# A graph network's last layer: a place of its own on chip for each tile's result, and all 25 stores behind the last gather

## The reference

```python
for l in range(3):
    ht = einsum('nd,rdo->nro', h, W_rel[l])              # 16 relations
    h_rel = segment_sum(ht[src, etype], dst) + h @ W_loop[l] + b_rel[l]
    z = (h @ W_gat[l]).reshape(n, 4, 32)                 # 4 heads
    e = leaky_relu(sum(z * attn_l[l], -1)[src] + sum(z * attn_r[l], -1)[dst], 0.2)
    alpha = softmax of e over the edges of each dst
    h_gat = segment_sum(alpha * z[src], dst).reshape(n, D) + b_gat[l]
    hc = concatenate([h_rel, h_gat], 1) @ W_fuse + b_fuse
    if l == 0: hc = hc * sigmoid(concatenate([hc, mean(edge_weight)], 1) @ W_gate + b_gate)
    h = relu(hc)
return layernorm(x + h)                                  # rows of 128, eps 1e-5
```

## Time and profile before

| | |
|---|---|
| median of 3 runs | 3509.68 us (3509.45 to 3509.83) |
| the profiled execution | 3503.46 us |
| its span, first to last instruction | 3501.9 us |
| last layer's first gather | 2402.68 us |
| last layer's last gather starts | 3467.19 us |
| in-loop stores of the last layer, first and last start | 2515.19 us, 3457.57 us |
| last store starts | 3494.12 us |

### The profile page before, as it was taken

One profiled execution on the slowest core, in us unless ns is written; L12 is line 12 of the kernel. 1 busy time (PEld: TensorE's weight loads), 2 busy tenths in 40 slices (PEclk: granted clock), 3 DMA queues, 4 the chain that ended last, 5 costly groups with the idle time before them and its releaser, 6 DMA issues.

```text
span 3501.9 us, 18300 instructions
## 1 busy us (share of the span) xinstructions
PE 679.2 (19%) x1897; PEld 366.6 (10%) x1897; DVE 2383.4 (68%) x3251; ACT 424.3 (12%) x769; POOL 2488.3 (71%) x2642
## 2 busy tenths in 40 slices
PE   8832111222222220101121112211000000000000
PEld 5421000111111110000000001100000000000000
DVE  8536666677667755666667766674777777877787
ACT  4530111011111110111011111111000000000000
POOL 1557777777777747777777777775777777777774
PEclk9965555555555665555555555555555555555555
DMA  7874545455555544545455555554333333333332
GB/s 280 335 227 129 152 129 152 152 152 152 152 161 166 151 158 106 153 129 152 152 152 152 152 152 163 163 157 133 105 104 106 104 105 105 104 105 105 104 105 65
DMA packets 143244, 505.96 MB, mean 144 GB/s; under 512 B 44277, under 2 KB 51002, under 8 KB 133618
## 3 DMA queue, kind: packets, MB, share of 16 engines
q0 software_dynamic: 130032, 444.45, 43.6%
q1 hardware_dynamic: 13186, 61.24, 4.5%
HBM read 341.05 MB, written 164.51 MB: 144 GB/s over the span
## 4 chain that ended last, share of the span: by engine, by line
POOL 44%; issue 29%; DVE 12%; DMA 6%; PE 3%; POOLq 3%; DVEq 1%; SPq 1%; ACT 1%; ACTq 0%
POOL meta_nat L596 20%; POOL late L596 13%; POOL scratch L596 11%; DVE acc L1381 4%; DMA table<-rows 2%; DVE scratch L1377 1%; DMA scratch<-table,stage_tail 1%; DVE meta_nat L1377 1%; DMA late<-table,stage_mid 1%; PE ps_table L885 1%; DVE late L1377 1%; DMA meta_nat<-table,stage_head 1%; POOLq L369 1%; POOL table L675 1%; PE ps_cnt L918 1%
## 5 line engine op out<-in xcount | busy, mean ns | idle before, releaser
L596 POOL DMA_INDIRECT meta_nat<-table,stage_head x1200 | 1137.7, 948 | 394.5 <-issue 385.6
L596 POOL DMA_INDIRECT late<-table,stage_mid x720 | 681.5, 947 | 219.3 <-issue 216.5
L596 POOL DMA_INDIRECT scratch<-table,stage_tail x555 | 525.6, 947 | 171.1 <-issue 171.1
L1024 PE MATMUL ps_mix<-ident,hr 128*128 128x128 f32 x75 | 35.5, 473 | 2017.4 <-DVE hg L1401 2017.4
L787 ACT ACTIVATE ps_cnt<-logit 128x68 f32<-128x68 f32 x189 | 43.7, 231 | 2792.8 <-DVE logit L1363 2791.7
L1381 DVE TENSOR_REDUCE acc<-meta_nat 128x132 f32<-128x2112 f32 x75 | 290.6, 3875 | 7.7
L1371 DVE TENSOR_REDUCE acc<-meta_nat 128x128 f32<-128x2048 f32 x75 | 282.8, 3770 | 0.0
L1048 PE MATMUL ps_table<-wrel,hT 128*128 128x512 f32 x400 | 265.2, 824 | 0.0
L1353 DVE TENSOR_TENSOR raw<-late,er_cur 128x64 f32<-128x64 f32 x45 | 12.0, 267 | 337.4 <-DMA late<-table,stage_mid 337.4
L1024 PEld LDWEIGHTS ps_mix<-ident,hr 128*128 128x128 f32 x75 | 13.6, 181 | 2066.0 <-DVE hg L1401 2066.0
L1381 DVE TENSOR_REDUCE acc<-scratch 128x132 f32<-128x1188 f32 (+1 forms) x69 | 208.7, 3024 | 7.1
(11 more groups left out here) (237 smaller groups left out, 1664.2 us busy)
## 6 DMA issues: line engine op xcount, KB each, us to landing
table<-rows SPq DMA_DIRECT2D x25, 2080.0 KB, 7.3
meta_nat<-table,stage_head POOLq DMA_INDIRECT x1200, 2.8
late<-table,stage_mid POOLq DMA_INDIRECT x720
scratch<-table,stage_tail POOLq DMA_INDIRECT x555, 2.8
meta<-meta_ranked SPq DMA_DIRECT2D x1, 2438.0 KB, 15.0
wrel<-in_L_gnn_W_rel POOLq DMA_DIRECT2D x2, 1024.0 KB, 13.3
meta_nat<-in_x SPq DMA_DIRECT2D x1, 832.0 KB, 19.4
table<-rows,stage_id POOLq DMA_INDIRECT x50, 7.8
```

Of the source, the lines that this page charges most:

```text
L596: pool.indirect_dma_start(out=slots[b][:, k, :], out_offset=None, in_=table[l % 2], in_offset=bass.IndirectOffsetOnAxis(ap=index, axis=0)) ...
L1024: pe.transpose(mix[0], hr[:], ident[:])
```

## The change

`yo` grows from one tile to 25 (`[P, T, D]`), so the scaling of tile t writes into a place of its own, given by a register, and no longer waits for the store before. The in-loop store of the last layer goes, with the wait for `s_yo` and `s_id` in front of it, and so do the two behind the loop. Behind the last layer's loop stand 25 stores, unrolled, each waiting for its tile's scaling; they read their node numbers straight from the columns of `id_u`, so the last layer no longer copies them into `stage_id`, nor waits for `s_stored` ahead of that copy. Layers 0 and 1 keep their stores. The same wait for all 26 landings ends the kernel.

```diff
-        yo = sb("yo", [P, D])
+        yo = sb("yo", [P, T, D])
...
-                if l < L - 1:
+                if nth:
+                    pool.wait_ge(s_rows, T + 1 + l * T + nth)
+                    pool.wait_ge(s_id, l * T + nth)
+                else:
                     pool.wait_ge(s_rows, n_rows_pool)
-                    pool.reg_add(n_rows_pool, n_rows_pool, 1)
-                else:
-                    pool.wait_ge(s_yo, nth or n_yo)
-                    pool.reg_add(n_yo, n_yo, 1)
-                pool.wait_ge(s_id, n_epi)
+                    pool.wait_ge(s_id, n_epi)
...
-                else:
-                    pool.indirect_dma_start(
-                        out=out, out_offset=bass.IndirectOffsetOnAxis(ap=stage_id[:], axis=0),
-                        in_=yo[:], in_offset=None, bounds_check=N - 1, oob_is_err=False).then_inc(s_out, 16)
-                    pool.reg_add(n_out_pool, n_out_pool, 16)
...
+            def store_result(t):
+                pool.wait_ge(s_yo, t + 1)
+                pool.indirect_dma_start(
+                    out=out, out_offset=bass.IndirectOffsetOnAxis(ap=id_u[:, t:t + 1], axis=0),
+                    in_=yo[:, t, :], in_offset=None, bounds_check=N - 1, oob_is_err=False).then_inc(s_out, 16)
...
-                with pool.If(t > 1):
-                    store_tile(l)
+                if l < L - 1:
+                    with pool.If(t > 1):
+                        store_tile(l)
...
-                store_tile(l, nth=T - 1)
-                store_tile(l, nth=T)
+                if l < L - 1:
+                    store_tile(l, nth=T - 1)
+                    store_tile(l, nth=T)
+            for t in range(T):
+                store_result(t)
             pool.wait_ge(s_out, 16 * (1 + T))
...
-                    dve.wait_ge(s_out, n_out)
-                    dve.reg_add(n_out, n_out, 16)
-                    v.tensor_scalar(yo[:], y[:], mv[:, 0:1], nv[:, 0:1], ALU.subtract, ALU.mult).then_inc(s_yo, 1)
+                    v.tensor_scalar(yo[:, bass.ds(t, 1)].rearrange("p o f -> p (o f)"), y[:], mv[:, 0:1], nv[:, 0:1],
+                                    ALU.subtract, ALU.mult).then_inc(s_yo, 1)
                 else:
                     dve.wait_ge(s_T, n_T)
                 if l < L - 1:
                     dve.reg_add(n_T, n_T, 1)
-                dve.wait_ge(s_stored, n_stored)
-                if l < L - 1:
+                    dve.wait_ge(s_stored, n_stored)
                     dve.reg_add(n_stored, n_stored, 16)
-                v.tensor_copy(stage_id[:].bitcast(I32), id_u[:, bass.ds(t, 1)].bitcast(I32)).then_inc(s_id, 1)
+                    v.tensor_copy(stage_id[:].bitcast(I32), id_u[:, bass.ds(t, 1)].bitcast(I32)).then_inc(s_id, 1)
```

More of the change, by code:

```diff
@@ L578, in _ @@
             n_stored_pool = counter(pool, "pool_stored", 16)
-            n_out_pool = counter(pool, "pool_out", 16)
             n_read = {b: counter(pool, f"pool_read_{b}", 1) for b in GROUPS}
@@ L583, in _ @@
             n_rows_pool = counter(pool, "pool_rows", T + 2)
-            n_yo = counter(pool, "pool_yo", 1)
             n_epi = counter(pool, "pool_epi", 1)
@@ L648, in next_block @@
                 pool.wait_ge(s_stored, n_stored_pool)
-                pool.wait_ge(s_out, n_out_pool)
                 with pool.If(first):
@@ L664, in store_tile @@
             def store_tile(l, nth=None):
-                if l < L - 1:
+                if nth:
+                    pool.wait_ge(s_rows, T + 1 + l * T + nth)
+                    pool.wait_ge(s_id, l * T + nth)
+                else:
                     pool.wait_ge(s_rows, n_rows_pool)
-                    pool.reg_add(n_rows_pool, n_rows_pool, 1)
-                else:
-                    pool.wait_ge(s_yo, nth or n_yo)
-                    pool.reg_add(n_yo, n_yo, 1)
-                pool.wait_ge(s_id, n_epi)
-                pool.reg_add(n_epi, n_epi, 1)
-                if l < L - 1:
-                    pool.indirect_dma_start(
[L676 to L679, removed]
-                else:
-                    pool.indirect_dma_start(
-                        out=out, out_offset=bass.IndirectOffsetOnAxis(ap=stage_id[:], axis=0),
-                        in_=yo[:], in_offset=None, bounds_check=N - 1, oob_is_err=False).then_inc(s_out, 16)
-                    pool.reg_add(n_out_pool, n_out_pool, 16)
+                    pool.wait_ge(s_id, n_epi)
+                pool.reg_add(n_rows_pool, n_rows_pool, 1)
+                pool.reg_add(n_epi, n_epi, 1)
+                pool.indirect_dma_start(
+                    out=table[(l + 1) % 2][0:NP_ * R, :].rearrange("(n r) f -> n (r f)", r=R),
+                    out_offset=bass.IndirectOffsetOnAxis(ap=stage_id[:], axis=0),
+                    in_=rows[0][:].rearrange("p r f -> p (r f)"), in_offset=None).then_inc(s_stored, 16)
+                pool.reg_add(n_stored_pool, n_stored_pool, 16)
+            def store_result(t):
+                pool.wait_ge(s_yo, t + 1)
+                pool.indirect_dma_start(
+                    out=out, out_offset=bass.IndirectOffsetOnAxis(ap=id_u[:, t:t + 1], axis=0),
+                    in_=yo[:, t, :], in_offset=None, bounds_check=N - 1, oob_is_err=False).then_inc(s_out, 16)
             def tile(l, t):
@@ L1315, in _ @@
             n_e = counter(dve, "v_epi", 1)
-            n_out = counter(dve, "v_out", 16)
             low = counter(dve, "v_low", 0)
```

## The result

| | before | changed |
|---|---|---|
| median | 3509.76 us (3509.45 to 3512.13, 4 runs) | 3491.19 us (3484.88 to 3493.14, 4 runs) |
| ratio | | 0.9942, 95% interval 0.9930 to 0.9954 |
| profiled execution, span | 3503.46 us, 3501.9 us | 3491.76 us, 3490.2 us |
| last layer's first gather to the span's end | 1099.2 us | 1078.4 us |

A forecast was written before the change was run, and what follows sets the result against it. GpSimd's descriptor work was taken to bound the last layer: -25.1 us up to the last gather and +6.0 us for the stores behind it make -19.1 us, from 3509.68 to 3490.6 us; range 3487.0 to 3497.5 us.

The forecast's parts named there:

- GpSimd's instruction stream is the pace: Last layer: GpSimd hardly ever waits, so each removed store gives 1.32 us; 18.5 us come off by tile 16.
- The late tiles give nothing: Tiles 16 to 24: new waits for VectorE's cast shrink the 11.9 us saved to 6.6 us.
- VectorE's own cycle of 33.4 us: Late tiles of the last layer: VectorE's work per tile, 11.3 + 5.9 + 11.6 + 4.3 + 0.3 us, is late next.
- the recursion: Order of tiles 16 to 24 computed with delays from the timeline; it matched the kernel before within 0.5 us.
- the 0.9 us rule: Head gathers begin no sooner than 0.9 us behind the head group's last VectorE instruction.
- VectorE's epilogue, 0.2 us shorter: Per tile of the last layer, the id copy and a little go: 0.2 us, bounds 0.3 us lost to 0.6 us gained.
- The burst: Behind the last gather: 24 stores at 1.32 us precede the last, 32.0 us against 26.0 before, giving back 6.0 us.
- The signs: Expected in the trace: last gather's end near 3443, last store's end near 3476, last scaling near 3468.
- (a): Last layer: VectorE's loop or the route from cast to first tail gather gets longer; 3492.4 to 3495.6 us, chance 0.14.
- (b): Route behind the cast 0.5 us shorter, stores at 1.27 us, or both with shorter VectorE tiles; 3487.3 to 3489.4 us, chance 0.10.
- (c): Last layer's gathers do not move up because something other than GpSimd's stream paces them; 3515.7 us, chance 0.05.
- (d): Stores at the end each wait for the one before to land, about 3.2 us each; 3535.7 us, chance 0.03.

The follow-up runs named there:

- twice_at_end: The changed kernel with each of the 25 stores at the end issued a second time, into a spare table: 3518.81 us, ratio 1.0033.

## Why the prediction was right

- **GpSimd's instruction stream is the pace, and a store taken out of it gives its whole price.** Right for tiles 2 to 20. The 14 tiles up to 15 gave 17.2 to 18.6 us where 18.5 were forecast, tiles 16 to 20 5.9 to 6.6 us where 6.3 were.
- **The late tiles give nothing.** Right in size: new waits of 1.2, 1.25, 2.3 and 1.8 us were forecast for tiles 21 to 24 and 0.9, 1.4, 2.1 (and 0.4 between two tail gathers) and 1.55 us over the ordinary gap were measured. Of the 0.45 us forecast before two head groups 0.3 us stand before the last one, and the 0.3 us of tile 16 came as 0.1 and 0.45 us. Tiles 21 to 23 kept their time within 0.2 us. Wrong in the party named: the text gave VectorE's own cycle of 33.4 us as what is late next. That holds for tile 21, whose time fell with a Newton step. In tiles 22 and 23 it is the cycle through the one head buffer, 33.9 us, which stood in the recursion as the 0.9 us rule but not in the sentence. The runs with fewer steps show it; with three steps tile 22 lies within 0.1 us of both.
- **VectorE's epilogue, 0.2 us shorter.** Right. From the sum of the head group to the next group 6.06 us passed before, and 5.87 us now:

```profile
3382.54 3.86 DVE L1381 TENSOR_REDUCE acc<-meta_nat 128x132 f32<-128x2112 f32 x1
...
3392.27 0.26 DVE L1353 TENSOR_TENSOR raw<-scratch,er_cur 128x60 f32<-128x60 f32 x1 [0.19 <-issue]
```

- **The burst.** The mechanism was right: 25 stores with no wait between them, ending behind VectorE's last result. The price was mis-sized: 1.32 us was taken and 1.293 us measured (0.983 us and the gap of 0.305 us), between the scatters that read a column of indices (1.27 us) and the slowest of the old stores (1.33 us), which had been the bounds. 24 stores make 0.65 us of it: +5.3 us in place of +6.0 us. The tail behind the last store is 0.4 us shorter, where no change was forecast. One term behind it was off without effect: VectorE was to need 25.0 us from the last gather's end to the last result and needed 26.1 us (3451.50 to 3477.62 us), so 5.2 us were to spare and not 6. 0.4 us of the difference are the last gather's, which comes sooner behind the tile's first gather. Another 0.4 us is a gap of 0.51 us in front of L1465, not explained by the trace, and 0.26 us lie in one copy, shown of the kernel before and then of the changed one. It runs beside a store (3460.94 us, 0.98 us long):

```profile
3477.69 0.29 DVE L1368 COPY scratch<-acc 128x260 f32<-128x260 f32 x1
```

```profile
3461.49 0.55 DVE L1368 COPY scratch<-acc 128x260 f32<-128x260 f32 x1
```

- **The signs.** The last gather's end, the last store and the last scaling came 8 to 10 us later than the places named, because the last layer began 9.1 us later. Counted from its first gather the last gather's end is 25.8 us sooner, where 25.1 us were forecast. "No gap above 0.31 us" in tiles 2 to 20 holds but for tile 16, where the prediction's own recursion had 0.3 us of wait.
- **Sum.** -19.1 us were forecast for the last layer and -20.8 and -19.0 us stand in the two pairs of traces; the medians give -18.6 and -21.4 us. The differences between these four lie in the scatter ahead of the last layer and in up to 0.1 us per tile within it. That the median came within 0.6 us of the forecast is luck in part: two traces of one kernel differ by more than that, and the prediction's stores were 0.65 us too dear in the burst.
- **Rivals.** (a) did not occur, and (b) only with half of the cheaper store: from the cast to the first tail gather it takes 1.5 us in the changed kernel's tiles 21 to 23 as before. It took 3.9 us in one tile of two other kernels, so (a) was a fair rival; what fills this time, which the prediction called sequencer time, no run shows. (c) is refuted by the periods of the tiles, (d) by the doubled burst. That the burst would be held up beside VectorE's copies is hardly seen either: its stores have a median of 0.983 us beside two epilogues, and only the first two (1.03 and 1.01 us) and the seventh (1.03 us) are longer. The seventh starts at 3459.61 us, while a scaling of VectorE (3459.44 us, 0.35 us long) is running, and takes 0.05 us more. In `twice_at_end` a store that starts beside a scaling as well (3455.86 us, the scaling 3455.72 us and 0.39 us long) takes 0.98 us. The Trainium skill, page "SBUF — State Buffer", section "Who interferes with whom", would have the one that comes second wait fully; no run here shows that in this direction. In the other direction the prediction read it out of one cast. The copy above is longer beside a store too, but the cast of tile 24 shown further up lies inside a store and takes 0.14 us, as in the changed kernel without one. So VectorE is held up beside a store at times, by up to 0.3 us here, and not always.

## What to carry to other kernels

An instruction is worth its price only where its engine never waits: read the gaps tile by tile, and expect the gain to end where a buffer's cycle or the partner's cycle is as long. Work that is moved behind a loop is free only up to the wait that stands there already; count both (here 26.0 us of wait took some 20 of 24 stores, the rest is paid in full). From then on a shorter last chain of another engine gives nothing. Where spans scatter by 10 us ahead of the change, compare the stretch that the change touches, from a common mark.

## What the runs showed of the hardware

- The time from the last store's end to the span's end differs with the kernel and repeats within 0.1 us between traces of the same arrangement of stores: 6.8 us before (three traces), 6.35 us with 25 stores at the end (four traces), 5.3 us with 12 (one), 7.5 us with 21 (two), 8.3 us with 22 (two), 8.7 us with 50 (one). It follows neither the number of stores nor their landing (2.2 to 3.2 us). What it is made of isn't shown by the profile.
- The time from a cast of VectorE to GpSimd's next gather, 1.5 us, became 3.9 us in one tile of two kernels in which a store is under way at the signal. With a store under way in tile 24 of the kernel before it took 1.8 us. It stays unexplained.
